# The second half of the value products is issued behind the first four transposes of the probabilities, in every attention tile

## The reference

```python
q = split_heads(query @ Wq.T + bq)      # query = layernorm(x)
k = split_heads(key @ Wk.T + bk)        # key = value = ctx
v = split_heads(value @ Wv.T + bv)
attn = jnp.einsum('bhsd,bhtd->bhst', q, k) / jnp.sqrt(jnp.float32(Hd))
attn = jax.nn.softmax(attn, axis=-1)    # the second attention masks keys first
out = jnp.einsum('bhst,bhtd->bhsd', attn, v)
out = out.transpose(0, 2, 1, 3).reshape(B, -1, D)
return out @ Wo.T + bo
```

## Time and profile before

| | |
|---|---|
| median of 3 runs | 1048.54 us (1046.0 to 1049.79) |
| the profiled execution | 1048.61 us, of which 1046.8 us are the span of the trace |
| PE busy | 971.6 us, 93% of the span |
| DVE, ACT, POOL busy | 848.1, 740.6, 587.6 us |
| steps of the first attention | from about 30 to 306 us |
| steps of the second attention | from about 545 to 840 us |

### The profile page before, as it was taken

The page is one execution under the profiler, slowest core; times in us unless marked ns, Lnnn a source line. Parts: engine busy times, 40 slices in busy tenths (PEclk is TensorE's granted clock), DMA queues, the critical chain, the costliest instruction groups (busy, mean ns, idle before and its releaser), DMA issues. The chain is left out here.

```text
span 1046.8 us, 36349 instructions
## 1 busy us (share of the span) xinstructions
PE 971.6 (93%) x11842; PEld 752.8 (72%) x11842; DVE 848.1 (81%) x2410; ACT 740.6 (71%) x1646; POOL 587.6 (56%) x1234
## 2 busy tenths in 40 slices
PE   2899999999889999999889999999999789999997
PEld 1577777777678999998866677777776567767675
DVE  3688888888848998889767888888877579999997
ACT  1687877778658777776647777777777567777774
POOL 4545446453206555556866444444443268888884
PEclk9999999999859999999999999999999799999999
DMA  2330110100000000000000000000000000000000
GB/s 84 105 106 21 41 36 24 40 10 21 12 2 1 1 0 0 0 0 1 1 11 13 22 12 19 14 16 18 12 10 3 1 6 24 20 23 20 23 20 29
DMA packets 19358, 21.48 MB, mean 21 GB/s; under 512 B 3552, under 2 KB 12000, under 8 KB 19296
## 3 DMA queue, kind: packets, MB, share of 16 engines
q1 hardware_dynamic: 19296, 20.68, 6.4%
HBM read 16.48 MB, written 4.19 MB: 20 GB/s over the span
## 5 line engine op out<-in xcount | busy, mean ns | idle before, releaser
L560 ACT ACTIVATE prob_t<-bank 128x512 f32<-128x512 f32 x256 | 152.8, 597 | 128.5 <-PE bank L1046 120.0
L770 DVE TENSOR_REDUCE smax<-score 128x16 f32<-128x1024 f32 x128 | 156.7, 1224 | 59.2 <-PE score L1078 46.9
L1046 PE MATMUL bank<-const,prob 128*128 128x128 f32 x1024 | 169.5, 289 | 16.4 <-ACT prob_t L560 16.4
L1101 PEld LDWEIGHTS bank<-vb,prob_t 128*64 128x64 f32 x4096 | 134.4, 142 | 49.4 <-issue 42.7
L555 ACT ACTIVATE prob<-prob 128x512 f32<-128x512 f32 x256 | 161.2, 630 | 10.6 <-DVE prob L779 9.7
L779 DVE TENSOR_TENSOR prob<-score,smax 128x512 f32<-128x512 f32 x256 | 164.7, 685 | 1.3
L1046 PEld LDWEIGHTS bank<-const,prob 128*128 128x128 f32 x1024 | 110.5, 143 | 70.5 <-issue 60.0
L1101 PE MATMUL bank<-vb,prob_t 128*64 128x18 f32 x4096 | 147.2, 215 | 0.0
L417 POOL TENSOR_SCALAR kj<-k_sb,const 128x512 f32<-128x512 f32 x128 | 88.1, 696 | 78.1 <-issue 39.3
L617 ACT ACTIVATE eb_t<-eb,gwt 128x128 f32<-128x128 f32 x256 | 81.4, 390 | 44.2 <-POOL eb_acc L433 28.6
L383 POOL TENSOR_TENSOR a_ve<-a_mv,const 128x4 f32<-128x4 f32 x32 | 6.5, 203 | 155.7 <-DVE a_mv L772 155.7
(11 more groups left out here) (146 smaller groups left out, 2386.3 us busy)
## 6 DMA issues: line engine op xcount, KB each, us to landing
ctx_t<-in_ctx SPq DMA_DIRECT2D x32, 256.0 KB, 2.6
x_all<-in_x SPq DMA_DIRECT2D x16, 256.0 KB, 2.8
out_x<-x_all SPq DMA_DIRECT2D x64, 64.0 KB, 1.5
ew<-in_ew SPq DMA_DIRECT2D x2, 512.0 KB, 4.4
f_cw<-in_f_cw SPq DMA_DIRECT2D x1, 768.0 KB, 7.1
w_t<-in_w_attn SPq DMA_DIRECT2D x2, 256.0 KB, 4.2
f_w<-in_f_w SPq DMA_DIRECT2D x2, 256.0 KB, 5.8
eb<-in_L_ffn_eb SPq DMA_DIRECT2D x1, 256.0 KB, 5.7
```

The costliest lines, as they stand in the source:

```text
L560: act.activation(prob_t[:, 4 * half:4 * half + 4, :].rearrange("p i q -> p (i q)"), bank[PT], ACT.Copy).then_inc(s["p_copied"], 1)
L770: dve.tensor_reduce(smax[:].rearrange("p (r h) -> p r h", r=RH), sc, AX.X, ALU.max).then_inc(s["smax_done"], 1)
L1046: return pe.transpose(dst, src, ident)
L1101: last = pe.matmul(bank[OV][q, i * 2 * VW:(i + 1) * 2 * VW], prob_t[:, i, q], vb[:, gp, v0 + b * NPAIR + i, :, :].rearrange("p h v -> p (h ...
```

## The change

In PE's step the 16 value products become two halves of 8: the first stands where all stood, the second moves behind the first four transposes. ACT's `copy_p(0)`, which writes over the first half of `prob_t` alone, now waits for the first half of the products through a new semaphore, `pv_lo`; `copy_p(1)` waits for the second half, as DVE's division does. No instruction that computes or copies is added or removed. The rest of the edit puts bodies of steps into named functions (of PE, ACT and DVE); DVE, POOL and SP have the same instructions in the same order with the same waits. Nothing is passed to the new parameter `beside`.

```diff
-                    def copy_p(half):
-                        wait(act, "pv_mm", n - 1)
-                        wait(act, "p_tr", 2 * (n - 1) + half + 1)
+            def copy_p(n, half):
+                wait(act, "pv_mm" if half else "pv_lo", n)
+                wait(act, "p_tr", 2 * n + half + 1)
...
+            def values_half(n, k, half):
+                v0 = k % G * BT * NPAIR
+                if half == 0:
+                    if k % G == 0:
+                        wait(pe, "v_ready", n + G)
+                    wait(pe, "o_norm", n)
+                wait(pe, "p_copied", 2 * n + half + 1)
+                for i in range(4 * half, 4 * half + 4):
+                    for b in range(BT):
+                        q = slice(b * S, (b + 1) * S)
+                        last = pe.matmul(bank[OV][q, i * 2 * VW:(i + 1) * 2 * VW], prob_t[:, i, q],
+                                         vb[:, k // G, v0 + b * NPAIR + i, :, :].rearrange("p h v -> p (h v)"),
+                                         start=True, stop=True, skip_group_check=True)
+                last.then_inc(s["pv_mm" if half else "pv_lo"], 1)
...
+                    split = True
                     if has(-2):
-                        gp = gpar if j >= 2 else 1 - gpar
...
-                        last.then_inc(s["pv_mm"], 1)
+                        values_half(n - 2, (k - 2) % 8, 0)
+                        if not split:
+                            values_half(n - 2, (k - 2) % 8, 1)
                     if has(-1):
-                        transpose_p(0)
+                        transpose_p(n - 1, (k - 1) % 8, 0)
+                    if has(-2) and split:
+                        values_half(n - 2, (k - 2) % 8, 1)
                     if has(-3):
```

More of the change, by code:

```diff
@@ L551, in step @@
                     o = 1 - par
[L552 to L555, removed]
-                    def copy_p(half):
-                        wait(act, "pv_mm", n - 1)
-                        wait(act, "p_tr", 2 * (n - 1) + half + 1)
-                        act.activation(prob_t[:, 4 * half:4 * half + 4, :].rearrange("p i q -> p (i q)"),
-                                       bank[PT], ACT.Copy).then_inc(s["p_copied"], 1)
                     if has(-1):
                         exponentials(n - 1, o, 1)
-                        copy_p(0)
+                        copy_p(n - 1, 0)
                     if has(-3):
[L568 to L573, removed]
+                        copy_o(L, n - 3)
                     if has(0):
@@ L600, in step @@
                         wait(act, "pv_mm", f - G)
[L601 to L605, removed]
-                return step
+                        copy_v(1 - gpar, bank[FRONT])
+                    if isinstance(t, int) and t in beside:
+                        beside[t]()
@@ L608, in experts, with normalise @@
+            def normalise(g, gp, tiles=range(G)):
+                wait(act, "m_ready", 4 * (g + 1))
+                wait(act, "mx_tr", g)
+                for j in tiles:
+                    act.activation(m_xn[:, j, :], x_tile(G * g + j), ACT.Identity,
+                                   bias=m_nr[:, gp, j:j + 1], scale=m_rs[:, gp, j:j + 1])\
+                        .then_inc(s["m_xn_ready"], 1)
             def experts(u, par, has):
                 o = 1 - par
[L611 to L618, removed]
@@ L783, in step @@
                     if has(-2):
[L785 to L793, removed]
@@ L796, in experts, with group_means, group_means_ready @@
+            def group_means(g, gp):
+                for j in range(G):
+                    dve.bn_aggr(m_mv[:, gp, j, :], m_st[:, gp, j, :]).then_inc(s["m_mean"], 1)
+            def group_means_ready(g):
+                wait(dve, "m_ready", 4 * (g - 1))
+                wait(dve, "m_ln", G * (g + 1))
             def experts(u, par, has):
                 o = 1 - par
[L801 to L826, removed]
-                                             scalar=gwt[:, o, j, e:e + 1], in1=src, op0=ALU.mult, op1=ALU.add)\
-                        .then_inc(s["y_v"], 1)
@@ L1052, in _, with transpose_p @@
             pe.wait_ge(s["ident16_done"], 1)
-            def attention(L):
+            def transpose_p(n, k, half):
+                wait(pe, "exp_done", 2 * n + half + 1)
+                wait(pe, "p_copied", 2 * n + half)
+                for i in range(4):
+                    c = (half * 4 + i) * P
+                    last = tr(bank[PT][:, i * P:(i + 1) * P], prob[:, k % 2, c:c + P])
+                last.then_inc(s["p_tr"], 1)
+            def values_half(n, k, half):
[12 more added lines that the diff above has]
+                last.then_inc(s["pv_mm" if half else "pv_lo"], 1)
@@ new lines, in values, with transpose_o, project_o @@
+            def values(n, k):
+                values_half(n, k, 0)
+                values_half(n, k, 1)
+            def transpose_o(n, k):
+                wait(pe, "o_norm", n + 1)
+                wait(pe, "x_attn", n)
+                tr(bank[OW][:, 0:P], o_n[:, k % 2, :]).then_inc(s["o_tr"], 1)
+            def project_o(L, n):
+                wait(pe, "o_copied", n + 1)
+                pe.matmul(bank[OW][:, P:2 * P], o_t[:], w_t[:, L, 3, :], start=True, stop=True)\
+                    .then_inc(s["wo_mm"], 1)
@@ new lines, in project_k, with project_q, project_v @@
+            def project_k(L, gp, dst):
+                pe.matmul(dst, w_t[:, L, 1, :], ctx_t[:, gp, :], start=True, stop=True).then_inc(s["k_mm"], G)
+            def project_q(L, dst):
+                pe.matmul(dst, w_t[:, L, 0, :], xn_t[:], start=True, stop=True).then_inc(s["q_mm"], G)
+            def project_v(L, gp, dst):
+                for i in range(G * BT):
+                    for h in range(2):
+                        last = pe.matmul(dst[h * S:(h + 1) * S, i * S:(i + 1) * S],
+                                         ctx_t[:, gp, i * S:(i + 1) * S], w_v[:, L, h, :],
+                                         start=True, stop=True, skip_group_check=True)
+                last.then_inc(s["v_mm"], G)
@@ L1134, in step @@
                     if has(-1):
-                        transpose_p(1)
+                        transpose_p(n - 1, (k - 1) % 8, 1)
                     if has(-3):
-                        wait(pe, "o_copied", n - 2)
-                        pe.matmul(bank[OW][:, P:2 * P], o_t[:], w_t[:, L, 3, :], start=True, stop=True)\
-                            .then_inc(s["wo_mm"], 1)
+                        project_o(L, n - 3)
                 return step
@@ new lines, in gate_mm, with transpose_mx @@
+            def gate_mm(u):
+                for j in range(G):
+                    last = pe.matmul(bank[FRONT][:, j * GW:(j + 1) * GW], mxt[:, j * P:(j + 1) * P], gate_w[:],
+                                     start=True, stop=True)
+                last.then_inc(s["gate_mm"], 1)
+            def transpose_mx(g):
+                wait(pe, "m_xn_ready", G * (g + 1))
+                wait(pe, "gate_v", GATE_STEPS * (g - 1) + 1)
+                for j in range(G):
+                    last = tr(bank[FRONT][:, j * P:(j + 1) * P], m_xn[:, j, :])
+                last.then_inc(s["mx_tr"], 1)
```

409 lines of the change are left out of this document (231 added, 178 removed).

## The result

| | before | after |
|---|---|---|
| median | 1048.53 us (5 runs) | 1061.65 us (1060.85 to 1063.66, 5 runs) |
| ratio to before | | 1.0131, 95% interval 1.0119 to 1.0142 |
| the profiled execution | 1048.61 us, span 1046.8 | 1060.85 us, span 1059.0 |

The change costs 13.1 us. 1064 was forecast, with a range of 1056 to 1069.

The account below looks back on a forecast made before the run. PE was taken to set the pace, except for waits for ACT. Borders +23.2, less 2.5, 0.7, 1.3, 1.2 and 2.0 given back, made +15.5 on 1048.6: 1064, range 1056 to 1069.

Parts of the forecast that it names:

- 0.27 a step: PE's added switch between 64-column and 128-column matmuls and back: 0.27 us a step, bounds 0.13 and 0.31, +23.2 in all.
- The three parts: Border cost on PE: 0.12 leaving the products, 0.06 for slower full matmuls behind them, 0.10 going back to half width.
- K and Q steps: Shorter wait for ACT's copy: 0.03 back in j=1 of both attentions and j=0 of the first, 42 steps, -1.3.
- j=3 steps: Steps transposing `a_xn`: -0.18 each in the second attention (-2.5), -0.05 in the first, limited by ACT (-0.7); 14 steps each.
- The work behind the first transposes: PE's work from first transposes to the others: more than 1.5 us in every step, so the 1.50 chain causes no wait.
- Steps 59 to 62: Second attention, with 59 and 60 of the first: the 0.89 wait goes, 0.33 less each, down to DVE's loop: -2.0.
- Hidden borders: Rival: PE loads weights of the other width ahead, switches cost nothing, only gains stay: -8.6, or 1040; chance 5%.
- The late second half as a chain: Rival: products, `o_n`, `o_t`, output projection, residual become a chain; 0.15 in 60 steps, +9: 1073; chance 5%.
- The clock: Rival: PE's 30 us half-clock stretch vanishes or another comes elsewhere, worth about 10: 1054 or 1074; 5% for either.

Follow-up runs that it names:

- a third block: Changed kernel with the second half of the products cut once more, the o_n transpose between the two pieces, in every step: 1082.29 us, ratio 1.0317 to before.
- v_step_border: Changed kernel with the split made only in the steps j=2, those with the V projection: 1055.60 us, ratio 1.0059 to before.
- the run with less work for ACT: Changed kernel without the second of ACT's two copies of V per group, half of the values missing: 1058.42 us, ratio 1.0093 to before.
- the twin of the V step: Changed kernel split only in V steps, with the second half of the products behind `o_n`, against the V projection: 1048.78 us, ratio 1.0000 to before.
- the kernel with the V step grouped: Kernel before, but in V steps the first transposes and o_n transpose precede the undivided products, which stand against the V projection: 1046.32 us, ratio 0.9970.
- the kernel with one border less: Changed kernel with the first transposes ahead of all 16 products, which stay one block: 1051.22 us, ratio 1.0020 to before.

## Why the prediction was right

The mechanism was the one foretold: PE sets the pace, each block of products costs its borders, and the wait for ACT gives back less. The forecast and the traces, by kind of step, over steps 2 to 58 (us):

| steps | first attention: forecast | measured | second: forecast | measured |
|---|---|---|---|---|
| 15 with V | +4.05 | +3.6 | +4.05 | +3.6 |
| 14 with K | +2.2 | +2.3 | +3.8 | +3.15 |
| 14 with Q | +3.4 | +2.8 | +3.4 | +2.8 |
| 14 with `a_xn` (j=3) | -0.7 | +0.2 | -2.5 | -2.7 |
| sum | +8.9 | +8.9 | +8.7 | +6.8 |

- **PE bounds, and the cost is borders.** Shown: a split without a border makes no difference, a third block adds 20.6 us more, and with the two borders and without the early transposes the V steps grow by 0.26 as they do here, and the time is 1093.
- **0.27 a step.** The V step shows it bare: 14 of the 15 V steps of each attention grew by 0.26, and the very first (step 2) did not grow. `v_step_border` cost 6.8 us, where 0.27 x 30 are 8.1. The three parts, 0.12 of the block, 0.06 behind it, 0.10 on the way back, stand in the rows after nearly as they were read: 0.12, 0.05, 0.09.
- **K and Q steps.** The 0.27 were to be eased by 0.03 in Q steps and in the K steps of the first attention, and by nothing in the K steps of the second. Most grew by 0.20. Timeline of PE in a Q step of the changed kernel:

```profile
612.56 1.02 PE L1154 MATMUL bank<-xn_t,w_t 128*128 128x512 f32 x2
613.42 0.60 PE L1105 MATMUL bank<-const,prob 128*128 128x128 f32 x4
```

  The others follow the projection after 0.86, where it was 0.89 (603.53 to 604.42), and their block lasts 0.60, where it was 0.63: the end of the wait was worth about twice the 0.03. In every second group the K steps were another matter: +0.25 in the second attention and less than 0.1 in the first, where PE had waited for DVE before. This is the mis-sized term; with the V steps it makes most of the 1.9 that the second attention is under the forecast.
- **j=3 steps.** In the second attention 4.26 became 4.04, near the -0.18 forecast (in every second group 4.35 became 4.18). In the first, ACT was named as the next limit and the step was to lose 0.05; it lost 0.03 and took 3.91, and the run with less work for ACT showed that it was ACT.
- **The sum of the first attention is right by luck.** One j=3 step, step 7, took 4.53 where it had taken 3.94: PE's scores stop there after 8 of 16 instructions and go on 0.84 behind their start (57.31, 58.15), with no engine named. The cause is open; the kernel with a single copy of V has it too (4.80), the one with the third block has not (3.98). This 0.6 happens to make up for V and Q steps that were counted too high.
- **The work behind the first transposes** was put at more than 1.5 in every step. Its terms (0.50 + 0.20 + 0.46 + 0.12 and 0.11 for `o_n`) make 1.39, and the trace has 1.33 (611.23 to 612.56). Where front work follows, it is enough. In a step without it the others still start 1.49 behind the first transposes (280.80 to 282.29), so the chain still holds them there, by about 0.16 us. The time was not touched: such steps lost up to 0.36, near the 0.33 forecast.
- **Outside the 57 steps** the span shrank by 3.5. Steps 59 to 62 of both attentions make 1.6 of it, where 2.0 were counted. Of the other 1.9, 1.3 lie behind step 63 of the second attention. PE ran at half clock there for 17.0 us before and for 13.6 in the changed kernel; the twin of the V step, whose list there is that of before, had 13.6 as well and was 1.1 shorter there. So this part need not be the change's doing. The start of the scores of step 2 scatters too: 36.44 in the twin and 37.67 in the kernel with the V step grouped, whose lists are the same up to there.
- **The rivals.** Hidden borders: excluded, every border cost. The prediction's own reading, that the weight loads in the trace run ahead and the gaps are there nevertheless, was only half right: they run ahead within a width, by 0.11, and not across a border, by 0.00. The late second half as a chain: excluded in the V step by the twin, where it ends latest at no cost, and made unlikely in the others by the kernel with one border less, whose products end about as late and which is 10 us shorter. The clock: the stretch at half clock at the end of the first attention lasted about 31 us in both kernels; where the borders stood alone PE spent about 14 us more at half clock there in the profiled execution, so the rival was real, in another kernel.
- **By the formula of the Trainium skill** ("TensorE: Matmul & The Clock Gate", Single matmul latency), which is given there for one bf16 matmul on the full array, the prediction had an estimate of 0.23 a step and a time of 1060, also close. The V steps measured 0.26, nearer to the 0.27 of the rows; the time of 1061.7 lies between the two sums because K and Q steps grew by less.

## What to carry to other kernels

Where PE is the bound, count how often its list passes between matmuls of different widths in the array, not only the matmuls: here each further half-width block between full-width ones cost 0.26 us, and moving one against another of its own shape gave 0.07 to 0.11 back a step (4.25 to 4.18 in the first attention, 4.57 to 4.46 in the second). An early release of another engine is worth only the wait that it ends; make such a move in those steps of a loop that wait, and leave the others. A rise of the busy share is no gain if the instructions are the same.

## What was not expected of the hardware

- A block of four products (8 instructions) pays as much at its borders as one of eight or sixteen: it takes 0.34 to its successor, of which four pairs are 0.23.
- Behind one full-width matmul that stands between two half-width blocks the next block starts 0.26 later, not 0.21, where five stand there: of what stands behind products, the second start was late by 0.05, in a block of transposes (0.66 instead of 0.60) as here.
- Weights are loaded 0.11 ahead of a full-width matmul that follows a full-width one, and 0.00 ahead (0.03 at most) at a passage between the widths.
- A matmul that waits shows the wait twice, in its start and in the spacing behind it: the block of four transposes lasts 0.63 and is followed after 0.47 where it waited (613.26, 613.73 before the change), and lasts 0.60 and is followed after 0.44 where it did not (622.29, 622.73 in the changed kernel).
